# Causal attention with two heads on the two 64-row halves of the tensor array, masks by small products, and one maximum instruction for two heads

## What is computed

```python
x = x + attn_a(layernorm(x), Wq, bq, Wk, bk, Wv, bv, Wo, bo)   # rope, 4 key/value heads shared by 4 heads each
x = x + ffn(layernorm(x), gate, up, down)                      # weights packed in 4 bits, with scales
x = x + attn_b(layernorm(x), Wq, Wk, Wv, Wo)                   # 16 key/value heads, no rope
x = x + ffn(layernorm(x), gate, up, down)
```

```python
scores = einsum('bthd,bshd->bhts', q, k) * scale
scores = where(causal, scores, -inf)
probs = softmax(scores, axis=-1)
out = einsum('bhts,bshd->bthd', probs, v)
```

## Time and profile before

| | |
|---|---|
| median of 3 runs | 2052.37 us (2046.72 to 2052.75) |
| span of the profiled execution, first to last instruction | 2051.7 us |
| attention a, 164 to 728 us of it | 564 us, PE busy 526.02, DVE 387.55, ACT 335.88 |
| attention b, 1157 to 1736 us of it (with 38.7 us in which PE waits for the loads) | 579 us, PE busy 518.66, DVE 382.35, ACT 304.34 |
| all other stages | 908.7 us |

### The profile page before, as it was taken

How to read it: one execution, slowest core, us unless ns; L and a number is a source line. 1 busy time by engine, 2 the same in 40 slices (tenths; PEclk the granted TensorE clock), 3 DMA queues, 4 the chain that set the end, 5 groups by cost and what they waited for, 6 DMA issues and landing times. The chain is left out here.

```text
span 2051.7 us, 27067 instructions
## 1 busy us (share of the span) xinstructions
PE 1763.2 (86%) x10026; PEld 1169.7 (57%) x10026; DVE 1238.4 (60%) x2979; ACT 915.3 (45%) x1274; POOL 468.9 (23%) x380
## 2 busy tenths in 40 slices
PE   2667999999999979999955368999999998899998
PEld 2444455555545357888844334555555544788887
DVE  4545877777776247444465257877777753654444
ACT  1111556665666724444321114555666565334333
POOL 2112323233334422232251140000000000123222
PEclk7665999999999989999988659999999999899999
DMA  4334002103010032000004631031030000500000
GB/s 122 94 107 88 20 35 62 49 24 90 20 39 20 31 160 103 1 0 0 0 0 157 206 95 35 1 58 26 1 82 1 1 1 29 218 11 1 10 10 10
DMA packets 67359, 103.68 MB, mean 51 GB/s; under 512 B 26128, under 2 KB 44304, under 8 KB 64976
## 3 DMA queue, kind: packets, MB, share of 16 engines
q1 hardware_dynamic: 63280, 85.84, 14.7%
q0 software_dynamic: 3968, 16.39, 2.1%
HBM read 61.84 MB, written 40.37 MB: 50 GB/s over the span
## 5 line engine op out<-in xcount | busy, mean ns | idle before, releaser
L952 ACT ACTIVATE probs<-ps_s 128x1024 f32<-128x1024 f32 (+3 forms) x640 | 547.1, 895 | 362.2 <-PE ps_s L900 182.3
L974 DVE TENSOR_REDUCE chunk_max<-ring 128x1 f32<-128x512 f32 x768 | 506.6, 686 | 134.6 <-PE ring L862 130.4
L862 PE MATMUL ring<-kt,qt 96*128 96x512 f32 (+3 forms) x1280 | 487.6, 430 | 76.6 <-PEq L400 58.5
L862 PEld LDWEIGHTS ring<-kt,qt 96*128 96x128 f32 x1280 | 232.9, 197 | 306.9 <-DVE chunk_max L974 117.3
L900 PE MATMUL ps_s<-qt,kt 128*128 128x512 f32 (+3 forms) x1280 | 374.5, 378 | 27.3 <-ACT qt L934 17.0
L1247 POOL TENSOR_TENSOR inter_lo<-inter,inter_hi 128x512 fp32r<-128x512 f32 x128 | 165.5, 1293 | 974.1 <-ACT inter_hi L1181 974.1
L977 DVE CUSTOM_DVE_ANT_0 masked<-ring,mask 128x384 f32<-128x384 f32 (+3 forms) x512 | 243.9, 486 | 126.0 <-PE ring L862 123.0
L920 PE MATMUL ps_o<-probs,vg 128*32 128x512 f32 (+3 forms) x2560 | 301.5, 544 | 0.0
L900 PEld LDWEIGHTS ps_s<-qt,kt 128*128 128x128 f32 x1280 | 229.1, 192 | 111.4 <-ACT probs L952 48.9
L1221 DVE SCALAR_TENSOR_TENSOR gelu_a<-gelu_a,ps_g 128x512 f32<-128x512 f32 x128 | 88.0, 687 | 185.9 <-ACT gelu_a L1175 185.6
L1175 ACT ACTIVATE gelu_a<-ps_g 128x512 f32<-128x512 f32 x128 | 76.6, 598 | 231.4 <-PE ps_u L93 231.1
(11 more groups left out here) (143 smaller groups left out, 2402.1 us busy)
## 6 DMA issues: line engine op xcount, KB each, us to landing
w_mlp<-w_scr SPq DMA_DIRECT2D x32, 768.0 KB, 14.7
w_scr<-w_parts POOLq DMA_DIRECT2D x16, 768.0 KB, 3.6
qt<-q_scr SPq DMA_DIRECT2D x24, 384.0 KB, 6.6
q_scr<-qk_hi SPq DMA_DIRECT2D x32, 256.0 KB
kt<-k_scr SPq DMA_DIRECT2D x18, 384.0 KB, 12.0
q_scr<-qk_lo SPq DMA_DIRECT2D x16, 256.0 KB
v_scr_b<-v_out SPq DMA_DIRECT2D x8, 512.0 KB, 9.5
k_scr<-qk_hi SPq DMA_DIRECT2D x16, 256.0 KB
```

Source lines behind the costliest of these rows:

```text
L862: pe.matmul(ring[n % 3][:, 0:w], qt[g][0:MROW, h // 2, q0:q0 + P], kt[g][(h // 2) % NKP][h % 2][0:MROW, c * TW:c * TW + w], start=True, st ...
L952: act.activation(pr[k % NPR][:, 2 * p:2 * p + 2, w0:TW], ps_s[p][:, :, 0:TW - w0], ACT.Exp, scale=SCALE).then_inc(s_e, 1)
L974: dve.tensor_reduce(dst, ring[n % 3][:, :], AX.X, ALU.max).then_inc(s_rd, 1)
```

## The change

1. A head of a pair now has one half of the array to itself: `qt` and `kt` hold the first head of the pair in rows 0 to 47 and the second in rows 64 to 111 (HALF = 64), and `kt` is one tensor for both. A matmul of M or S takes 48 or 49 rows of one half, in a tile of 64 rows by 128 columns. The two matmuls of a pair name different halves and different PSUM banks.
2. An M step is now for a pair: two matmuls into a slot of two banks (`ring`, two slots instead of three of one bank), and one maximum of VectorE over 2 x 512 columns. There are 80 of them in a group; LEAD and LEAD0 are halved.
3. The masks of M are added by PE too: four products of 64 rows by 128 columns on each diagonal M, so the custom instruction of VectorE is gone. On a diagonal S the masks are four such products instead of two of 128 rows.
4. `ps_s` has three single banks instead of two of two banks (NSB = 3). ScalarE takes the exponential of one head at a time, 512 columns in an instruction. An S of a pair waits until the exponentials are done up to the second last head before it.
5. R and T go through `ring`. The maxima of a tile are copied by ScalarE into a small tensor `row`, two buffers, and SP copies them with a DMA into rows 48 and 112 of `qt`; the first S of a tile waits for that DMA. `kt` has ones in all rows but the keys', so only one memset is left.
6. SP's list is now: the DMA of each R in order, and behind the one of tile 0 of group g the loads of group g + 1, with their wait. The loads of the packed chunks have gone to ScalarE's queue, behind Y.

```diff
@@ the S step on the tensor engine
-                    pe.wait_ge(s_e, last_user(x))
-                    if kb == 0 and p == 0:
-                        pe.wait_ge(s_e, scored[("R", g, t)] + 1)
+                    m = scored(g, t, kb, 2 * p)
+                    if m + 2 > NSB:
+                        pe.wait_ge(s_e, m + 2 - NSB)
+                    if kb == 0 and p == 0:
+                        k = rows[("R", g, t)]
+                        pe.wait_ge(s_row[k % 2], 16 * (k // 2 + 1))
                     w0 = width(t, kb)
+                    diagonal = kb >= BT * t
                     for h in range(2):
-                        last = pe.matmul(ps_s[p][:, h, 0:TW - w0], kt[g][p % NKP][h][:, kb * P:(kb + 1) * P],
-                                         qt[g][:, p, t * TW + w0:(t + 1) * TW],
-                                         start=True, stop=kb < BT * t)
+                        op = pe.matmul(ps_s[(m + h) % NSB][:, 0:TW - w0], kt[g][shifted[h], p % NKP, kb * P:(kb + 1) * P],
+                                       qt[g][shifted[h], p, t * TW + w0:(t + 1) * TW],
+                                       start=True, stop=not diagonal)
+                        if not diagonal:
+                            op.then_inc(s_s, 1)
+                    if diagonal:
+                        for a in range(2):
+                            for h in range(2):
+                                op = pe.matmul(ps_s[(m + h) % NSB][:, 0:P], ident[half[h], a, :], below[half[h], a, :],
+                                               start=False, stop=a == 1)
+                                if a == 1:
+                                    op.then_inc(s_s, 1)
@@ the M step
+                out = ring[n % 2]
+                for h in range(2):
+                    last = pe.matmul(out[:, h, 0:w], qt[g][plain[h], p, q0:q0 + P],
+                                     kt[g][plain[h], p % NKP, c * TW:c * TW + w], start=True, stop=c < t)
+                if c == t:
+                    for a in range(2):
+                        for h in range(2):
+                            last = pe.matmul(out[:, h, w - P:w], ident[half[h], a, :], above[half[h], a, :],
+                                             start=False, stop=a == 1)
+                dve.tensor_reduce(mp[t % 2][:, qb, 2 * p:2 * p + 2, c], ring[n % 2][:, :, 0:w], AX.X, ALU.max).then_inc(s_rd, 1)
@@ SyncE
+            for x, k in rows.items():
+                _, g, t = x
+                sp.wait_ge(s_ra, by_act[x] + 1)
+                sp.dma_start(qt[g][QROWS:QROWS + HALF + 1:HALF, :, t * TW:(t + 1) * TW].bitcast(F32),
+                             row[k % 2][:, :, :].bitcast(F32)).then_inc(s_row[k % 2], 16)
+                if t == 0 and g + 1 < NG:
+                    if g:
+                        sp.wait_ge(s_pv, pvs[("PV", g - 1, NT - 1, NB - 1)] + 1)
+                    heads.load_q(sp, (g + 1) % 2, g + 1, s_qk[(g + 1) % 2])
+                    heads.load_k(sp, (g + 1) % 2, g + 1, s_qk[(g + 1) % 2])
+                    heads.load_v(sp, (g + 1) % 2, g + 1, s_vg[(g + 1) % 2])
@@ the exponential on ScalarE
-                    act.activation(pr[k % NPR][:, 2 * p:2 * p + 2, w0:TW], ps_s[p][:, :, 0:TW - w0], ACT.Exp,
-                                   scale=SCALE).then_inc(s_e, 1)
+                    for h in (2 * p, 2 * p + 1):
+                        m = scored(g, t, kb, h)
+                        act.wait_ge(s_s, m + 1)
+                        act.activation(pr[k % NPR][:, h, w0:TW], ps_s[m % NSB][:, 0:TW - w0], ACT.Exp,
+                                       scale=SCALE).then_inc(s_e, 1)
```

More of the change, by code:

```diff
@@ L44 @@
 SCALE = HD ** -0.5
-NEG_BIG = -3.0e38
 VC = 32
@@ L147, in _ @@
-            pool.wait_ge(s_m, 6)
+            pool.memset(per["half_ident"][:, :, :], 0.0).then_inc(s_m, 1)
+            for name, far in (("above", (0, 1)), ("below", (1, 0))):
+                for a in range(2):
+                    for h in range(2):
+                        pool.memset(per[name][:, a, h * HALF:(h + 1) * HALF], MASKED if (a, h) == far else 0.0).then_inc(s_m, 1)
+            pool.wait_ge(s_m, 12)
             pool.affine_select(out=ident[:, :], in_=ident[:, :], compare_op=ALU.not_equal, fill=1.0,
@@ L787, in attention_phase @@
         NPR = 3
+        NSB = 3
         pr = [t_.sb(f"probs{i}", [P, GH, TW]) for i in range(NPR)]
-        junk = [t_.sb(f"masked{i}", [P, TW]) for i in range(3)]
         mp = [t_.sb(f"chunk_max{i}", [P, BT, GH, NT]) for i in range(2)]
         neg = [t_.sb(f"neg_max{i}", [P, BT, GH]) for i in range(2)]
+        row = [t_.sb(f"max_row{i}", [2, 2, TW], F32R) for i in range(2)]
         ot = t_.sb("o_t", [P, TW])
@@ L853, in _ @@
-            for j in range((NG - 1) * (NF // NG), NF if extra else 0):
-                dq.load(sp, j)
+            for x, k in rows.items():
[9 more added lines that the diff above has]
+                    heads.load_v(sp, (g + 1) % 2, g + 1, s_vg[(g + 1) % 2])
@@ L899, in _ @@
                     for h in range(2):
-                        last = pe.matmul(ps_s[p][:, h, 0:TW - w0], kt[g][p % NKP][h][:, kb * P:(kb + 1) * P],
-                                         qt[g][:, p, t * TW + w0:(t + 1) * TW],
-                                         start=True, stop=kb < BT * t)
-                    if kb >= BT * t:
-                        for h in range(2):
-                            last = pe.matmul(ps_s[p][:, h, 0:P], per["ident_bf"][:, :], per["mask_t"][:, :],
-                                             start=False, stop=True)
```

263 lines of the change are left out of this document (122 added, 141 removed).

## The result

The changed kernel takes 2194.47 us, the median of 4 runs from 2175.26 to 2207.03, beside 2052.56 for the kernel before. The ratio is 1.0678, with a 95% interval from 1.0614 to 1.0742: slower by 142 us, where 53 were forecast. The profiled execution spans 2184.2 us, and its mean granted clock is 0.853, where before it was 0.924.

What follows compares the result with a forecast made beforehand. The prediction took packed PE to bound the attention, and after the change the chain through the first head's exponential. Layer b +22.5, layer a +18.5 and clock +12 gave +53, hence 2106 us; range 2025 to 2240.

Steps and rivals of the forecast that it cites:

- The row: Tile 1, groups 1 and 2: PE waits for maxima DMA behind loads, 10.5 us in layer a, 17 in b; 55 total.
- Rival 1: The rows' DMA isn't held back and may land after 3 us; 55 and 12 go, 2040 us; chance 0.13.
- The halves: S and M pairs: both matmuls run at once on two row halves, four slots of 0.23 us a block, not eight.
- Rival 3: Pairs on the halves don't run at once: 3.3 us a block, +130, 2236 us; chance 0.10.
- The chain: Full blocks: second S waits for the first head's exponential, so a block takes 2.83 us instead of 3.07.
- Rival 2: The chain is shorter or doesn't end last; blocks at PE's 2.37 us, 1960 us with the stalls; chance 0.09.
- Layer a's extras: Layer a: Y, three DMA issues and T's copy on ACT cost 0.5 to 1 us more a chunk, +10 us.
- Group 0: Group 0, where DVE bounds: cheaper M were to save 10 us in layer b and 9 in layer a.
- The clock: After each row stall PE begins at half clock: two blocks at 4.3 instead of 2.83 us, +12 in all.
- rival 4: Clock stays at 1.2 GHz after pauses or falls between; a third of blocks at 4.3 us, +155, 2260 us; chance 0.15.
- The last tile: Last tile of group 3, without M: full blocks go from PE's packed 2.1 us to the chain's 2.6, +5 us.
- PE's busy time: Sign in the profile after: PE's busy time falls by more than 100 us although the span grows.

Runs made afterwards that it cites:

- e1: Changed kernel with the row DMA of tile 1 in groups 1 and 2 sent ahead of the next group's loads: 2120.03 us, ratio 1.0306.
- e6: e1 with layer a's packed-weight loads issued by SP again instead of ACT: 2103.54 us, ratio 1.0232.
- e8: e1 with a useless pair of matmuls ahead of each M pair between a block's two S: 2090.25 us, ratio 1.0163.
- e2: Changed kernel with a useless pair of 512-column matmuls behind each S in the last tile of group 3: 2168.51 us, ratio 1.0582.
- e7: e5 and e6 combined, with last-tile scores of group 3 in the ring's double slots and one exponential of 1024 columns: 2019.77 us, ratio 0.9820.
- e9: e5 with all mask products left out, for maxima and scores: 2065.84 us, ratio 1.0047.
- e3: Changed kernel with two M instead of one between the two S of a block: 2143.62 us, ratio 1.0429.
- e5: Changed kernel with the edits of e1 and e3 together: 2062.77 us, ratio 1.0041.

## Why the prediction was right and wrong

The forecast was 53 us, as 55 for the row, 12 for the clock and -14 for all the rest. Measured were 142: slower as forecast, and inside the wide range (2025 to 2240), but 89 us above the forecast.

**The row: right.** Named with its place, twice in each layer, 10.5 and 17 us each; measured 12 and 20, 65 in all. Rival 1 had it landing in time; its issue alone stood for 16.55 us. The DMA carries 8 KB, not the 16 that the rival names. A smaller wait was put at nothing: the row's own way hides "under the block that lies between R and S" but for tile 2 of group 0, where there is no such block and PE waits 3.0 us instead of 1.2 before.

**The halves: right.** Rival 3 (not at once) is out: a pair takes 0.50 us from start to end, and S and M pairs end 0.24 apart (1536.12 and 1536.36), against the slot of 0.23 that the sum used.

**The chain: right in kind, 0.08 us short.** It sets the block, by the exponential of the first head: 2.91 us where 2.83 were forecast, since the second S begins 0.08 later: ACT begins 0.10 us behind the end of the first S (1536.12 to 1536.22), and 0.03 were taken. Rival 2 (PE alone, 2.37) is out: tiles 0 to 3 of layer b's middle groups at the full clock are 10.7, 23.5, 36.2 and 50.9 us (e1, groups 1 and 2, and for tile 3 group 2 of the changed kernel), 121.3 in sum, where "121 to 122 us" was written. DVE's busy time fell by 67, about 60 was written; a maximum of 1024 columns takes 1.22 us, 1.14 was written.

**Layer a's extras: of the right kind.** ACT's issues and copies stand on the path as written (+10); e6 moved the issues and gained 16, the clock in it.

**Group 0: too hopeful.** In place of -10 in layer b and -9 in layer a its tiles are -0.8 and +6.5. In them 73 us more are at 0.50 than before, 38 of them behind the two waits of 3.0 us for the row of tile 2.

**The clock: the term that failed.** The step reads "After such a pause PE begins at half clock [...]; two blocks at 4.3 (below) instead of 2.83 are 3 us each: +12". So the sum lets the clock fall behind four waits only and come back after two blocks. At these four places the term is right: tile 1 behind each wait lost 3.2 us (26.7 and 23.5, 27.6 and 24.4 us, changed and e1). It failed by what it leaves out: everywhere else the clock was put at nothing. That a block "leaves PE idle for 0.5 of 2.83 us" stands in rival 4 alone, at 0.15. What the trace has is 642 us at 1.2 GHz instead of 312. Of the 330 more, 95 lie at the four waits for the row (tiles 0 and 1 of groups 1 and 2), 90 in the two last tiles, 73 in group 0, and 72 in the other tiles, 58 of them in layer a, behind pauses of 1.8 to 2.8 us for ACT.

How much time it costs can be read from runs of one kernel: the four of the changed kernel go from 2175.3 us at a mean clock of 0.855 to 2207.0 at 0.836, that is 31.8 us for 93 us more at 1.2 GHz, 0.34 each. The blocks say the same: 4.13 instead of 2.67 is 0.35 of each us. The mean of the four is 0.846, 675 us at 1.2 GHz, 363 more than before; less the 65 in which PE stands still anyway, by 0.34, it is an estimated 100 us (77 to 116 by the slopes of the other kernels' runs, 0.26 to 0.39). Rows 65, clock 100 and a rest of -23, which is what is left over and not measured, make the 142; the forecast had 55, 12 and -14.

e8, which adds work, shortens no chain and saves 30 us with 87 less at 1.2 GHz (0.34 of 87 is 30), shows that the clock is a cause of its own and not only a mark of the waits; e2 shows it in its tile. The measured time lies within rival 4's bounds, and what happened is the forecast with a good part of rival 4 on top. Rival 4's picture, a clock that falls in the full blocks themselves, isn't what the trace has: these stand at 1.00 in most of layer b. It falls behind longer pauses, and where a tile has no M it comes back late (layer a) or not at all (layer b).

**The last tile** is the clearest case of that term. The prediction made it +5 by the chain alone, and it was +30.7 in layer b and +13.5 in layer a. By 0.35 of its 66 us some 23 of layer b's are the clock, an estimate. The prediction's own numbers held a warning: a block without M has the same chain, 2.6 us, and 1.9 of it are work (0.33 + 0.23 + 0.33 + 1.00).

**What was to be seen.** PE's busy time was to fall by more than 100 us and fell by 54, because the instructions at 1.2 GHz are longer in it: a pair of S 0.79 us instead of 0.50, in the rows of the last tile above. Busy time is no measure of work where the clock moves. The sign that did tell was the last one of the prediction, the granted clock of the attentions: not near 0.95 but 0.85 in both layers (before: 0.98 and 1.00).

The Trainium skill has the pattern: TensorE: Matmul & The Clock Gate (A second HAM failure mode: psum-queue depth-cycling) tells of a kernel whose clock went back and forth because PE paused between groups of matmuls for its PSUM banks. This trace agrees in part. PE pauses for a bank in each block, and 330 us more are at half clock, in 23 stretches behind the first scores of the two attentions, where before there were 2; but the full blocks with a pause of 0.51 us run at 1.00 in most of layer b, and what stands in front of most falls is one longer pause. The short ones matter behind it, in the last tile of layer b: with them the clock stayed at 0.50, and with a useless pair in each (e2) or without them (e7) it came back.

## What to carry to other kernels

When a change makes PE wait where it was packed, price not only the chain but every block at both levels of the clock: here that is 2.67 against 4.13 us. Look for the single longer pauses that set it off, behind another engine's extra work or a small DMA, and for stretches in which PE has nothing to fill its pauses with, where it may not come back. Work taken from PE in such a state bought nothing here (e9) until the waits were filled or removed; independent work put into the gap (e3) filled them, and more banks where they are free (e7) removed them. And where a small transfer that the next step waits for shares a queue with bulk loads, issue it first: one line gave 74 us.

## What the runs showed of the hardware

- Useless matmuls shortened a kernel: a pair in each gap by 30 us (e8), with the chain no shorter; 64 pairs brought a tile's clock from 0.50 to 1.00 and the tile from 66.1 to 52.4 us (e2).
- The same blocks, each with a pause of 0.74 us, ran at 1.00 for 13 us (2.67 us each) and, behind one pause of 1.88 us, at 0.50 (4.13 us each).
- Leaving out all mask products, 2048 of them, changed the time by 3 us while the mean granted clock went from 0.868 to 0.838 (ten runs each).
- The same kernel, in runs on one chip, differs by 7 to 32 us, and its mean granted clock goes with it: 2053.3 us at 0.874 and 2076.4 at 0.860 for e5. The kernel before stays within 14 to 20 us over 13 runs, at 0.918 to 0.929. Differences under some 15 us between two such versions were not to be read from a few runs.
- Two matmuls on 64-row halves take 0.50 us for 512 columns, and a pair every 0.24, by the side of 0.23 for one matmul on 96 or 128 rows before.
